# Summing the weighted experts of the last three groups on VectorE in one operation each, instead of on GpSimd in three additions

## The chip, the cores and the metric

The kernel runs on one core of a Trainium2 chip. The metric is the device time of one execution in microseconds (us), the median of several runs. The core's engines work side by side, each through its own list of instructions in order, and they wait for one another on semaphores: TensorE (PE in the profile) for matrix products, VectorE (DVE), ScalarE (ACT), GpSimd (POOL), and SyncE (SP), which here only issues DMAs.

## What is computed

An image of 160 x 160 tokens with 64 channels goes through one block: attention along each row, then a mixture of experts for each token. Cut to what matters:

```python
x = x + attention(layernorm(x))            # 4 heads of 32, a bias from the tokens, gates
t = to_tokens(x)                           # 25600 tokens of 64 channels
h = layernorm(t)
router_probs = softmax(h @ router_w + router_b)            # 8 experts
top_p, top_i = top_k(router_probs, 2)
top_p = top_p / sum(top_p)
expert_out = einsum("bnd,edc->bnec", h, expert_w) + expert_b
out = t + einsum("bnk,bnkc->bnc", top_p, gather(expert_out, top_i))
```

The kernel computes all 8 experts of every token and weights them with a table of coefficients that holds zero for the six that were not chosen. Summing the 8 weighted experts of a token is the part that the change touches.

## The kernel before

The 160 rows of the image are cut into 40 groups (GROUPS) of 4 rows, that is 640 tokens: 5 slabs (T, numbered t) of 128 tokens, one token to a partition. A first phase of about 80 us normalizes all tokens. After it every engine runs the same written list of steps, n = -2 to 43. In step n an engine works on up to six groups at different stages: the scores of group n and n+1, the attention output of group n-1, router, coefficients and the first experts of group n-2, the other experts of group n-3, and the result of group n-4. The list in each engine's own `step(n, a)` is the order; nothing reorders it. From step 37 on the steps are written out (they are not in the loop), and from step 40 on no new group comes in, so a step holds less and less: group 37 ends in step 41, group 38 in step 42, group 39, the last, in step 43. These last steps are called the drain here.

The way of one group g through its last stages:

- `attention_out` (VectorE, L864) adds the projected attention to the input: x1. `total2` (L870) and `mean2` (L875) follow, GpSimd's `center` (L395) subtracts the mean, ScalarE squares, `sumsq2` (VectorE, L882) sums, GpSimd's `norm2` takes the power (L376) and multiplies (L379), ScalarE and `low2` (GpSimd, L406) make the halves, and TensorE turns them over (`turn2`, L1004). ScalarE copies them out, and TensorE computes the router and the experts of the slabs.
- `logits` (VectorE, L889), twelve small operations `route` (L898 to L910), an exponential on ScalarE, and `share` 1 to 5 (L921 to L928) give the coefficients. All are chained: each waits for the one ahead.
- `weigh` (VectorE, L944) multiplies the 8 x 64 experts' values of a slab, read from PSUM, by the coefficients, into a buffer `prod` in SBUF. Slab 2 takes another way: ScalarE copies it to `kept`, and GpSimd weighs it (`weigh_kept`, L423).
- GpSimd sums the 8 experts of a slab in three additions, 8 to 4 (`mix_halves`, L429), 4 to 2 (L434) and 2 to 1 (L436), both in `mix_rest`; the sum goes to `ymix`.
- `residual` (GpSimd, L443) adds x1 and the five slabs of ymix to `base`. `finish` (VectorE, L953) adds the experts' bias, and SyncE stores the result.

Two more things on GpSimd's list matter below: `og_low` (L417) makes the low halves of the gated attention output, without which TensorE cannot project it (`project_out`, L1236 to L1238), and `residual`. In the list of a step both stand behind the additions of the step before. VectorE's gated outputs come from `gated` (L849) and `normed` (L857), and TensorE's spreading of the inverse sums stands between these two.

Of the kernel before, what the change touches and what calls it, by code (L numbers as in the profile page):

```python
# [5 lines left out]
ALU = mybir.AluOpType  # L6
ACT = mybir.ActivationFunctionType
AX = mybir.AxisListType
# [37 lines left out]
def build(nc, x, Wq, Wk, Wv, Wg, Wo, Wb, router_w, router_b, expert_w, expert_b, mask, out):  # L46
    with ExitStack() as ctx:
# [145 lines left out]
        def pairs_loop(eng, body, first, end):  # L193

            with eng.Fori(0, (end - first) // 2) as i:
                body(i * 2 + first, first % 2)
                body(i * 2 + (first + 1), 1 - first % 2)
# [23 lines left out]
        def on(g):  # L221

            return not isinstance(g, int) or 0 <= g < GROUPS

        def later(g):

            return on(g) and not (isinstance(g, int) and g == 0)

        N_WLOAD = 2 * 6 + 1 + T + 3 * T


        @KE.sync
        def _(sp):
            def at(g, size):

                return g * size if isinstance(g, int) else sp.snap(g * size)

            def load_x(m, a):
                start = at(m, 2 * TG * D)
                need(sp, lnA, 3 * m - 3)  # L240
                sp.dma_start(xin[a][:], x_flat[bass.ds(start, 2 * TG * D)].rearrange("(p t d) -> p t d", p=P, t=T2)
                             ).then_inc(x_loaded[a], 16)

            def keep_xs(m, a):
                start = at(m, 2 * TG)
                sp.wait_ge(xs_made, m + 1)
                sp.dma_start(xs_all[:, bass.ds(start, 2 * TG)], xs_pair[a][:]).then_inc(xs_kept[a], 16)

            for m in range(2):
                load_x(m, m)  # L250
            for half_ in range(2):
                sp.dma_start(w_raw[64 * half_:64 * half_ + 64, B0:B0 + 4], Wb).then_inc(wb_loaded, 16)
            ld = lambda dst, src: sp.dma_start(dst, src).then_inc(w_loaded, 16)

            for half_ in range(2):
                rows = slice(64 * half_, 64 * half_ + 64)
                ld(w_raw[rows, V0:V0 + 128], Wv)
                ld(w_raw[rows, G0:G0 + 128], Wg)
                ld(w_raw[rows, X0:X0 + 512].rearrange("p (e c) -> p e c", e=E), expert_w.rearrange("e d c -> d e c"))
                ld(w_raw[rows, R0:R0 + 8], router_w)  # L260
                ld(w_raw[rows, Q0:Q0 + 128], Wq)
                ld(w_raw[rows, K0:K0 + 128], Wk)
                load_x(2 + half_, half_)
            ld(w_raw[:, O0:O0 + 64], Wo)
            load_x(4, 0)
            for t in range(T):
                ld(rb[:, t, :], router_b.rearrange("(a e) -> a e", a=1).broadcast_to([P, E]))
            load_x(5, 1)
            keep_xs(0, 0)
            load_x(6, 0)  # L270
            keep_xs(1, 1)
            sp.wait_ge(const_ready, 1)

            def load_eb(part):
                for t in range(T):
                    ld(eb_raw[40 * part + 8 * t:40 * part + 8 * t + 8, t, :], expert_b)

            load_eb(0)
            load_x(7, 1)
            keep_xs(2, 0)  # L280
            load_eb(1)
            load_x(8, 0)
            keep_xs(3, 1)
            load_eb(2)

            def load_xq(g, a):
                start = at(g, TG)
                for k in range(2):
                    for c in range(2):
                        need(sp, qk_done[k][c], g - 1)  # L290
                sp.dma_start(xs_q[a][:], xs_all[:, bass.ds(start, TG)]).then_inc(xq_loaded[a], 16)

            def load_xv(g, a):
                start = at(g, TG)
                need(sp, v_done, g - 1)
                need(sp, vr_done, g - 1)
                for c in range(2):
                    need(sp, g_done[c], g - 1)
                sp.dma_start(xs_v[a][:], xs_all[:, bass.ds(start, TG)]).then_inc(xv_loaded[a], 16)

            def phase1(n, a):
                load_x(n + 2, a)
                keep_xs(n - 3, 1 - a)

            pairs_loop(sp, phase1, 7, PAIRS - 3)
            for n in range(PAIRS - 3, PAIRS + 4):
                if n + 2 < PAIRS: load_x(n + 2, n % 2)
                if n - 3 < PAIRS: keep_xs(n - 3, 1 - n % 2)
                if n == PAIRS:
                    sp.wait_ge(xs_kept[0], 16)  # L310
                    for g in range(2):
                        load_xq(g, g)
            def load_res(g, a):
                start = at(g, TG * D)
                need(sp, x1_done, g - 1)
                sp.dma_start(xin[a][:, 0:T], tokens(x_flat, start)).then_inc(x_loaded[a], 16)

            def store(g, a):
                start = at(g, TG * D)
                sp.wait_ge(res_done, g + 1)  # L320
                sp.dma_start(tokens(out_flat, start), res[a][:]).then_inc(res_stored[a], 16)

            for a in range(2):
                sp.wait_ge(xs_kept[a], 16 * (PAIRS // 2))
            load_xv(0, 0)
            load_res(0, 0)
            load_xv(1, 1)
            load_res(1, 1)

            def step(n, a):  # L330
                b = 1 - a
                if on(n + 3): load_xq(n + 3, b)
                if isinstance(n, int) and n < 1: return
                if on(n + 1): load_xv(n + 1, b)
                if on(n - 4): store(n - 4, a)
                if on(n + 1): load_res(n + 1, b)

            for n in range(-1, LOOP):
                step(n, n % 2)
            pairs_loop(sp, step, LOOP, LOOP_END)  # L340
            for n in range(LOOP_END, LAST):
                step(n, n % 2)
            for a in range(2):
                sp.wait_ge(res_stored[a], 16 * (GROUPS // 2))

# [2 lines left out]
        def _(pool):  # L348
# [95 lines left out]

            def step(n, a):
                b = 1 - a
                if on(n - 4): mix_rest(n - 4, 3)
                if on(n - 4): mix_rest(n - 4, 4)
                if on(n - 2): og_low(n - 2, 1)
                if on(n - 2): og_low(n - 2, 0)  # L450
                if on(n - 4): residual(n - 4, a)
                if on(n - 1): rinv_low(n - 1)
                if on(n - 3): mix_halves(n - 3, 0)
                if on(n - 2): center(n - 2, a)
                if on(n - 3): weigh_kept(n - 3, 2)
                if on(n - 2): norm2(n - 2, a)
                if on(n - 3): mix_halves(n - 3, 1)
                if on(n - 2): low2(n - 2, a)
                if on(n - 3): mix_rest(n - 3, 1)
                if on(n - 3): mix_rest(n - 3, 0)  # L460
                if on(n - 3): mix_halves(n - 3, 2)
                if on(n - 3): mix_halves(n - 3, 3)
                if on(n - 3): mix_rest(n - 3, 2)
                if on(n - 3): mix_halves(n - 3, 4)

            run_steps(pool, step)

# [191 lines left out]
        def _(dve):  # L659
# [276 lines left out]
            def weigh(g, t, bank):  # L936
# [6 lines left out]
                else: need(dve, mix_step[WEIGHED[i::2][-1]], 3 * (g - 1) + 1)  # L943
                dve.scalar_tensor_tensor(out=prod_of(t)[:], in0=bank[:].rearrange("p (e c) -> p e c", e=E), scalar=1.0 / UP,  # L944
                                         in1=coef[:, t, :].unsqueeze(2).broadcast_to([P, E, D]),
                                         op0=ALU.mult, op1=ALU.mult).then_inc(prod_done[t], 1)

            def finish(g, a, bank):

                dve.wait_ge(cb_done, g + 1)  # L950
                dve.wait_ge(base_done, g + 1)
                need(dve, res_stored[a], 8 * g - 8 * a)
                dve.scalar_tensor_tensor(out=res[a][:], in0=bank[:, 0:T * D].rearrange("p (t d) -> p t d", t=T), scalar=1.0 / UP,  # L953
                                         in1=base[:], op0=ALU.mult, op1=ALU.add).then_inc(res_done, 1)

            def step(n, a):
# [5 lines left out]
                if on(n - 1): normed(n - 1, 0, ps_x)  # L962
                if on(n - 1): normed(n - 1, 1, ps_o)
                if on(n - 3): weigh(n - 3, 3, ps_m)
                for k in range(6, 8):
                    if on(n - 3): share(n - 3, k)
                if on(n - 3): weigh(n - 3, 4, ps_o)
                if later(n + 2): qk_low(n + 2, a, 1, 0, ps_m)
                if later(n + 2): qk_low(n + 2, a, 0, 0, ps_x)
                if on(n + 1): row_max(n + 1, 1)  # L970
# [15 lines left out]
                    if on(n - 2): share(n - 2, k)  # L986
                if on(n - 1): total2(n - 1, b)
                if on(n - 2): weigh(n - 2, 0, ps_m)
                if on(n - 1): mean2(n - 1, b)
                if later(n + 2): qk_low(n + 2, a, 0, 1, ps_x)  # L990
                if on(n + 2): row_max(n + 2, 0)
                if on(n - 1): sumsq2(n - 1, b)
                if on(n - 2): weigh(n - 2, 1, ps_r)

            run_steps(dve, step)


# [340 lines left out]
```

## Time and profile before

| what | value |
|---|---|
| median of three runs | 909.1 us (908.54 to 911.25) |
| the profiled execution | 911.06 us, its span 909.2 us |
| mean granted TensorE clock | 0.974 of full speed |
| VectorE busy | 760.7 us, 84% of the span |
| GpSimd busy | 641.0 us, 71% of the span |
| TensorE busy | 812.7 us, 89% of the span |

The span reaches from the first to the last instruction of the trace; all times of instructions below are counted from its start. In the steps of the middle a step takes about 19 us. The drain takes up the last 45 us.

### The profile page before, as it was taken

The page shows a single profiled execution, that of the slowest core. Times are in us where ns is not written, and L with a number is a line of the kernel's source. Part 1 is how long each engine was busy: PE and PEld are TensorE (multiplying, and loading weights), DVE is VectorE, ACT ScalarE, POOL GpSimd, SP SyncE. Part 2 cuts the span into 40 slices and gives each one's busy share as a digit, 9 for nine tenths or more (in the row PEclk, how much of TensorE's full clock was granted, in tenths as well). Part 3 has the DMA queues.
Part 4 walks back from the last instruction along what each step waited for, and adds up shares of the span by engine and source line. Part 5 has one row for each costly group of instructions (what it writes and reads, how often), then busy time and mean ns, then how long its engine had stood idle before and what let it go on. Part 6 is the DMA issues. An engine that isn't in the chain of part 4 may idle for free.

```text
span 909.2 us, 40901 instructions
## 1 busy us (share of the span) xinstructions
PE 812.7 (89%) x15532; PEld 536.6 (59%) x15532; DVE 760.7 (84%) x1818; ACT 485.4 (53%) x1049; POOL 641.0 (71%) x1029
## 2 busy tenths in 40 slices
PE   1999678999999999999999999999999999999743
PEld 1898345656656566665666656666666666656421
DVE  8998445898898898988989989899888998898764
ACT  3886235555565555655456554555546555565410
POOL 6994002677777677776777767777677777777786
PEclk9999989999999999999999999999999999999975
DMA  4563000011110011001110011100101001100000
GB/s 126 192 197 134 19 18 25 25 31 54 39 32 30 29 50 36 29 29 34 45 36 29 29 39 40 36 29 29 45 34 36 29 29 50 36 23 25 17 14 16
DMA packets 32461, 40.82 MB, mean 45 GB/s; under 512 B 6288, under 2 KB 27280, under 8 KB 32400
## 3 DMA queue, kind: packets, MB, share of 16 engines
q1 hardware_dynamic: 31920, 39.95, 13.3%
q8 instruction: 43, 0.70, 0.3%
q14 instruction: 18, 0.15, 0.1%
q10 hardware_dynamic: 480, 0.02, 0.0%
HBM read 13.74 MB, written 6.55 MB: 22 GB/s over the span
## 4 chain that ended last, share of the span: by engine, by line
PE 36%; DVE 35%; issue 19%; POOL 7%; ACT 1%; DVEq 1%; DMA 0%; POOLq 0%; ACTq 0%
DVE negm L826 6%; PE psS L1113 6%; DVE rinv L842 5%; PE psS L1088 5%; DVE prod L944 3%; POOL ln_s L376 3%; PE ps_o L1170 3%; PE ps_x L1173 2%; PE ps_x L1170 2%; PE ps_o L1173 2%; DVE og L857 2%; DVE rt L906 2%; DVE q_lo L778 2%; POOL xn L379 2%; DVE ogu L849 2%
## 5 line engine op out<-in xcount | busy, mean ns | idle before, releaser
L429 POOL TENSOR_TENSOR add<-prod 128x256 f32<-128x256 f32 x160 | 116.5, 728 | 100.4 <-DVE prod L944 100.4
L826 DVE TENSOR_REDUCE negm<-psS 128x12 f16<-128x1920 f32 x80 | 146.0, 1825 | 12.8 <-PE psS L1098 7.9
L376 POOL TENSOR_TENSOR ln_s<-ln_s,half 128x5 f32<-128x5 f32 (+1 forms) x60 | 86.2, 1436 | 38.6 <-DVE ln_s L882 30.8
L434 POOL TENSOR_TENSOR add<-add 128x128 f32<-128x128 f32 x200 | 91.4, 457 | 0.1
L602 ACT ACTIVATE hl<-xn 128x320 f16<-128x320 f32 x40 | 18.8, 470 | 129.4 <-POOL xn L379 129.4
L546 ACT ACTIVATE pt_b<-psS 128x1920 f32<-128x1920 f32 x40 | 70.9, 1771 | 18.9 <-PE psS L1132 15.1
L411 POOL TENSOR_TENSOR rinv_lo<-rinv,rinv_hi 128x160 f16<-128x160 f32 x40 | 19.8, 496 | 83.8 <-ACT rinv_hi L577 83.8
L436 POOL TENSOR_TENSOR ymix<-add 128x64 f32<-128x64 f32 x200 | 64.4, 322 | 15.7
L1088 PE MATMUL psS<-bm,ident 128*128 128x480 f16 (+1 forms) x320 | 68.4, 336 | 7.0 <-ACT pt_a L546 3.1
L417 POOL TENSOR_TENSOR og_lo<-og,og_hi 128x320 f16<-128x320 f32 x80 | 61.8, 794 | 17.0 <-ACT og_hi L583 17.0
L1113 PE MATMUL psS<-bt_hi,ident 128*128 128x320 f16 (+1 forms) x320 | 68.5, 337 | 2.3 <-DVE negm L826 2.3
L857 DVE TENSOR_TENSOR og<-ogu,ps_x 128x320 f32<-128x320 f32 x40 | 19.5, 487 | 51.5 <-issue 48.9
L553 ACT ACTIVATE v_main<-ps_x 128x512 f32<-128x512 f32 x40 | 23.9, 598 | 65.9 <-PE ps_x L1184 65.9
L379 POOL TENSOR_TENSOR xn<-xc,ln_s 128x320 f32<-128x320 f32 (+1 forms) x60 | 54.2, 904 | 5.3 <-POOL ln_s L376 1.1
L1113 PE MATMUL psS<-bt_lo,ident 128*128 128x320 f16 x320 | 57.7, 303 | 0.0
L596 ACT ACTIVATE sq<-xc 128x320 f32<-128x320 f32 x40 | 18.9, 471 | 72.0 <-POOL xc L395 72.0
L944 DVE SCALAR_TENSOR_TENSOR prod<-ps_m,coef 128x512 f32<-128x512 f32 x80 | 54.7, 684 | 2.8 <-PE ps_m L1246 2.7
L1236 PE MATMUL ps_m<-w_hi,og_hi 128*128 128x64 f16 x200 | 28.1, 208 | 30.1 <-DVE rinv L842 22.4
L546 ACT ACTIVATE pt_a<-psS 128x1280 f32<-128x1280 f32 x40 | 49.5, 1237 | 3.8 <-PE psS L1122 3.8
L1088 PEld LDWEIGHTS psS<-bm,ident 128*128 128x128 f16 x320 | 27.2, 98 | 36.6 <-ACT pt_a L546 22.1
L842 DVE RECIPROCAL rinv<-ps_m 128x160 f32<-128x160 f32 x40 | 45.8, 1145 | 1.7 <-PE ps_m L1146 1.7
L1236 PEld LDWEIGHTS ps_m<-w_hi,og_hi 128*128 128x128 f16 x200 | 24.0, 128 | 37.4 <-DVE rinv L842 18.7
(279 smaller groups left out, 2979.5 us busy)
## 6 DMA issues: line engine op xcount, KB each, us to landing
xin<-in_x SPq DMA_DIRECT2D x20, 320.0 KB, 3.0
xs_all<-xs_pair SPq DMA_DIRECT2D x20, 320.0 KB, 2.5
xs_q<-xs_all SPq DMA_DIRECT2D x40, 160.0 KB, 2.1
xs_v<-xs_all SPq DMA_DIRECT2D x40, 160.0 KB, 2.1
xin<-in_x SPq DMA_DIRECT2D x40, 160.0 KB, 2.2
out<-res SPq DMA_DIRECT2D x40, 160.0 KB, 1.8
w_raw<-in_expert_w SPq DMA_DIRECT2D x2, 128.0 KB
eb_raw<-in_expert_b SPq DMA_DIRECT2D x15, 2.0 KB
```

Source lines behind the costliest of these rows:

```text
L376: pool.tensor_tensor(ln_s[a][:, 3, 0:w], ln_s[a][:, 2, 0:w], half[:, 0:w], ALU.pow).then_inc(own, 1)
L379: pool.tensor_tensor(xn[a][:, 0:w], xc[a][:, 0:w], ln_s[a][:, 3, 0:w].unsqueeze(2).broadcast_to([P, w, D]), ALU.mult).then_inc(own, 1)
L417: pool.tensor_tensor(og_lo[:, cols], og[:, cols], og_hi[:, cols], ALU.subtract).then_inc(ogl_done[c], 1)
L429: pool.tensor_tensor(add1[t % 2][:], prod_of(t)[:, 0:4, :], prod_of(t)[:, 4:8, :], ALU.add).then_inc(mix_step[t], 1)
L434: pool.tensor_tensor(add2[t % 2][:], add1[t % 2][:, 0:2, :], add1[t % 2][:, 2:4, :], ALU.add).then_inc(mix_step[t], 1)
L436: pool.tensor_tensor(ymix[:, t, :], add2[t % 2][:, 0, :], add2[t % 2][:, 1, :], ALU.add).then_inc(mix_step[t], 1)
L546: act.activation(pt[:].rearrange("p h s i -> p h (s i)"), psS[:, :, 0:slots * N], ACT.Exp).then_inc(exp_done[c], 1)
L826: dve.tensor_reduce(negm[c][:, :, 0:slots], psS[:, :, 0:slots * N].rearrange("i h (s j) -> i h s j", s=slots), AX.X, ALU.max, negate=True) ...
L842: dve.reciprocal(rinv[:], bank[:, 0:N]).then_inc(rinv_done, 1)
L944: dve.scalar_tensor_tensor(out=prod_of(t)[:], in0=bank[:].rearrange("p (e c) -> p e c", e=E), scalar=1.0 / UP, in1=coef[:, t, :].unsqueeze ...
L1088: mm(psS[:, h, 0:(3 - c) * N], lhsT=ident16[:], rhs=bm3[:, h].rearrange("i s j -> i (s j)")[:, 0:(3 - c) * N], start=True, stop=False)
L1113: mm(psS[:, h, 0:wide], lhsT=ident16[:], rhs=part[:, h].rearrange("j s i -> j (s i)")[:, 0:wide], start=part is bt3_hi, stop=False)
```

## The change

For groups 37, 38 and 39 (`late(g)`), GpSimd's `mix_halves` and `mix_rest` are left out. In their place VectorE sums a slab by one `tensor_reduce` over the experts (`mix_late`), which reads the buffer through a rearranged view, with the expert innermost. The weighted values of one token lie in SBUF as 8 rows of 64 floats, so neighbouring reads of this view are 64 floats (256 bytes) apart. `mix_late` counts the slab's semaphore up by 3, as the three additions did. `weigh_kept` of slab 2 stays on GpSimd. The edits to SyncE's part only write the same list in another way.

```diff
+        LATE = GROUPS - 3
+        def late(g):
+            return isinstance(g, int) and LATE <= g < GROUPS
+        def early(g):
+            return on(g) and not late(g)
...
 # GpSimd's step
-                if on(n - 4): mix_rest(n - 4, 3)
-                if on(n - 4): mix_rest(n - 4, 4)
+                if early(n - 4): mix_rest(n - 4, 3)
+                if early(n - 4): mix_rest(n - 4, 4)
...
-                if on(n - 3): mix_halves(n - 3, 0)
+                if early(n - 3): mix_halves(n - 3, 0)
...
 # VectorE
+            def mix_late(g, t):
+                dve.wait_ge(prod_done[t], g + 1)
+                need(dve, base_done, g)
+                dve.tensor_reduce(ymix[:, t, :], prod_of(t)[:].rearrange("p e c -> p c e"), AX.X, ALU.add).then_inc(mix_step[t], 3)
...
                 if on(n - 3): weigh(n - 3, 3, ps_m)
+                if late(n - 3): mix_late(n - 3, 3)
                 for k in range(6, 8):
                     if on(n - 3): share(n - 3, k)
                 if on(n - 3): weigh(n - 3, 4, ps_o)
+                if late(n - 3): mix_late(n - 3, 4)
+                if late(n - 3): mix_late(n - 3, 2)
...
                 if on(n - 2): weigh(n - 2, 0, ps_m)
+                if late(n - 2): mix_late(n - 2, 0)
...
                 if on(n - 2): weigh(n - 2, 1, ps_r)
+                if late(n - 2): mix_late(n - 2, 1)
```

What this does to the lists of instructions is shown at two places. First GpSimd, from the `low2` of group 39 in step 41 to the end of its list. Before:

```order
L406 TENSOR_TENSOR hl<-xn,hl 128x5x64
L434 TENSOR_TENSOR add<-add 128x128
L436 TENSOR_TENSOR ymix<-add 128x64
...
L443 TENSOR_TENSOR base<-ymix,x_0 128x320
L429 TENSOR_TENSOR add<-prod 128x256
L423 TENSOR_TENSOR kept<-kept,coef 128x512
L429 TENSOR_TENSOR add<-prod 128x256
L434 TENSOR_TENSOR add<-add 128x128
...
L443 TENSOR_TENSOR base<-ymix,x_1 128x320
```

In the changed kernel (line numbers are 8 higher there):

```order
L414 TENSOR_TENSOR hl<-xn,hl 128x5x64
L451 TENSOR_TENSOR base<-ymix,x_0 128x320
L431 TENSOR_TENSOR kept<-kept,coef 128x512
L451 TENSOR_TENSOR base<-ymix,x_1 128x320
```

All additions L429, L434 and L436 of these groups are gone, 15 to a group; both `residual` (base) have nothing ahead of them any more but what VectorE delivers.

Second VectorE, from the last coefficients of group 39 in step 41 to the end of its list. In the changed kernel, where L952 is `weigh`, L960 the new sum, L967 `finish`, L939 and L941 are `share` 6 and 7:

```order
L936 TENSOR_TENSOR coef<-rt,rs 128x40
L952 SCALAR_TENSOR_TENSOR prod<-ps_m,coef 128x512
L960 TENSOR_REDUCE ymix<-prod 128x64
L952 SCALAR_TENSOR_TENSOR prod<-ps_r,coef 128x512
L960 TENSOR_REDUCE ymix<-prod 128x64
L967 SCALAR_TENSOR_TENSOR res<-ps_m,base 128x320
L952 SCALAR_TENSOR_TENSOR prod<-ps_m,coef 128x512
L960 TENSOR_REDUCE ymix<-prod 128x64
L939 CAST c_stack<-coef 128x2x40
L941 TENSOR_TENSOR c_stack<-coef,c_stack 128x40
L952 SCALAR_TENSOR_TENSOR prod<-ps_o,coef 128x512
L960 TENSOR_REDUCE ymix<-prod 128x64
```

One more L960 (of `kept`) and the last `finish` follow. Before, the same list stands there without the five sums. In steps 39 and 40 the sums stand in the same places behind their `weigh`, so that what follows in the list, `mean2`, `gated`, `share` and `logits` among it, comes behind them.

## Rows read from the trace of the kernel before

**Rows 1.** The page's first part: busy us, share of the span, instructions.

```profile
PE 812.7 (89%) x15532; PEld 536.6 (59%) x15532; DVE 760.7 (84%) x1818; ACT 485.4 (53%) x1049; POOL 641.0 (71%) x1029
```

**Rows 2.** The chain of work that ended last: start us, us, what.

```profile
900.22 0.44 PE ps_m L1259 x5
900.66 5.76 issue
906.42 0.49 DVE res L953
```

**Rows 3.** Timeline of GpSimd in the drain: start, us, line, out<-in, idle before.

```profile
863.84 0.72 POOL L395 TENSOR_TENSOR xc<-x,ln_s 128x320 f32<-128x320 f32 x1
...
875.16 1.56 POOL L417 TENSOR_TENSOR og_lo<-og,og_hi 128x320 f16<-128x320 f32 x2
...
880.30 0.72 POOL L429 TENSOR_TENSOR add<-prod 128x256 f32<-128x256 f32 x1 [2.76 <-DVE prod L944]
880.99 0.72 POOL L395 TENSOR_TENSOR xc<-x,ln_s 128x320 f32<-128x320 f32 x1
...
892.57 0.86 POOL L443 TENSOR_TENSOR base<-ymix,x 128x320 f32<-128x320 f32 x1 [0.26 <-POOL ymix L436]
...
904.25 0.32 POOL L436 TENSOR_TENSOR ymix<-add 128x64 f32<-128x64 f32 x1
905.12 0.86 POOL L443 TENSOR_TENSOR base<-ymix,x 128x320 f32<-128x320 f32 x1 [0.55 <-POOL ymix L436]
```

**Rows 4.** Timeline of VectorE in the drain, with the same columns.

```profile
862.98 0.16 DVE L875 TENSOR_SCALAR ln_s<-ln_s 128x5 f32<-128x5 f32 x1
...
869.87 0.68 DVE L944 SCALAR_TENSOR_TENSOR prod<-ps_o,coef 128x512 f32<-128x512 f32 x1
871.55 0.20 DVE L889 TENSOR_TENSOR lg<-ps_x,rb 128x40 f32<-128x40 f32 x1 [1.01 <-PE ps_x L1226]
...
876.27 0.48 DVE L921 TENSOR_SCALAR rs<-rs 128x5 f32<-128x5 f32 x1 [0.28 <-ACT rs L615]
876.78 0.19 DVE L922 RECIPROCAL rs<-rs 128x5 f32<-128x5 f32 x1
877.83 0.49 DVE L864 SCALAR_TENSOR_TENSOR x<-ps_m,xin 128x320 f32<-128x320 f32 x1 [0.86 <-PE ps_m L1238]
...
879.53 0.69 DVE L944 SCALAR_TENSOR_TENSOR prod<-ps_m,coef 128x512 f32<-128x512 f32 x1 [0.20 <-PE ps_m L1246]
880.14 0.16 DVE L875 TENSOR_SCALAR ln_s<-ln_s 128x5 f32<-128x5 f32 x1
...
885.47 0.82 DVE L931 CAST c_stack<-coef 128x80 f16<-128x80 f32 x1
...
889.28 0.20 DVE L889 TENSOR_TENSOR lg<-ps_x,rb 128x40 f32<-128x40 f32 x1 [1.99 <-PE ps_x L1226]
...
892.63 0.85 DVE L909 TENSOR_TENSOR rt<-rt,rs 128x40 f32<-128x40 f32 x1
...
893.96 0.17 DVE L921 TENSOR_SCALAR rs<-rs 128x5 f32<-128x5 f32 x1 [0.27 <-ACT rs L615]
...
899.27 0.68 DVE L944 SCALAR_TENSOR_TENSOR prod<-ps_o,coef 128x512 f32<-128x512 f32 x1
```

**Rows 5.** Stretches of VectorE from `logits` to `share` 1 (steps 40, 41): us, busy (instructions), clock.

```profile
871.55:876.27 4.72, 4.03 (x14) 0.65 0.00 0
889.28:893.96 4.68, 4.00 (x14) 0.50 0.01 4
```

**Rows 6.** All 40 instructions of one line of `route`: ns min/median/max, first and last start.

```profile
L909 DVE TENSOR_TENSOR rt<-rt,rs x40: 199/200/850, 165.1 to 892.6; 128x40 f32<-128x40 f32 x40
```

**Rows 7.** VectorE's reductions by shape: count, busy us, mean ns, idle before.

```profile
L870 DVE TENSOR_REDUCE ln_s<-x 128x5 f32<-128x320 f32 x40 | 19.2, 480 | 0.0
...
L734 DVE TENSOR_REDUCE ln_s<-xin 128x10 f32<-128x640 f32 x20 | 16.3, 814 | 1.7 <-DMA xin<-in_x 1.5
...
L685 DVE TENSOR_REDUCE fold<-ident 128x32 f32<-128x128 f32 x1 | 0.4, 356 | 0.0
```

More of the change, by code:

```diff
@@ L227, in later, with third_on @@
             return on(g) and not (isinstance(g, int) and g == 0)
+        LATE = GROUPS - 3
[3 more added lines that the diff above has]
+            return on(g) and not late(g)
+        def third_on(g):
+            return on(g) and not (isinstance(g, int) and g < 2)
         N_WLOAD = 2 * 6 + 1 + T + 3 * T
@@ L331, in step @@
                 b = 1 - a
-                if on(n + 3): load_xq(n + 3, b)
-                if isinstance(n, int) and n < 1: return
-                if on(n + 1): load_xv(n + 1, b)
+                if third_on(n + 3): load_xq(n + 3, b)
+                if third_on(n + 1): load_xv(n + 1, b)
                 if on(n - 4): store(n - 4, a)
[L336 to L342, printed above, removed]
+                if third_on(n + 1): load_res(n + 1, b)
+            run_steps(sp, step)
             for a in range(2):
@@ L456, in step @@
                 if on(n - 2): norm2(n - 2, a)
-                if on(n - 3): mix_halves(n - 3, 1)
+                if early(n - 3): mix_halves(n - 3, 1)
                 if on(n - 2): low2(n - 2, a)
[L459 to L464, printed above, removed]
+                if early(n - 3): mix_rest(n - 3, 1)
+                if early(n - 3): mix_rest(n - 3, 0)
+                if early(n - 3): mix_halves(n - 3, 2)
+                if early(n - 3): mix_halves(n - 3, 3)
+                if early(n - 3): mix_rest(n - 3, 2)
+                if early(n - 3): mix_halves(n - 3, 4)
             run_steps(pool, step)
```

## The prediction

> **What bounds the kernel now.** I read four views, from the whole to the end of the program. The page's first part shows TensorE, VectorE and GpSimd busy for 89%, 84% and 71% of the span [rows 1]; these are averages over all steps, and the change touches only the last three groups. Nothing ahead of 863 us moves: the first new sum stands in step 39, behind the `weigh` that `mean2` at 862.98 follows. So the question is what sets the time of the last 45 us.
>
> The chain of work that ended last closes with TensorE's bias product at 900.22, a piece called "issue" of 5.76 us, and the last `finish` at 906.42 [rows 2]. The piece is not idle in truth. GpSimd's timeline shows what runs beside it: the last of the additions of group 39 starts at 904.25 and `residual` at 905.12, for 0.86 us [rows 3]. VectorE's last `weigh` began at 899.27 [rows 4], so 7.15 us pass from there to `finish`, and GpSimd fills them.
>
> GpSimd's queue shows a second wait. The additions of group 37 stand ahead of `og_low`, which starts at 875.16 [rows 3]. TensorE's projection waits for it, and VectorE's `attention_out` sits idle for 0.86 us before 877.83 [rows 4]. Elsewhere in the drain the path runs through VectorE: a round goes from `logits` over `route` and `share`, `attention_out`, `weigh`, `mean2`, then GpSimd's `center` and norm, TensorE's turn and router, to the next `logits` at 889.28 [rows 4]. The last group is VectorE alone from 889.28 to 899.27.
>
> The third thing to see is the small operations of `route`. One has a median of 200 ns over 40 executions, but a maximum of 850 ns, at 892.6 [rows 6]. That one starts at 892.63 and ends at 893.48, while GpSimd's `residual` runs from 892.57 to 893.43 [rows 3, 4]: it ends right behind it. So an operation on two SBUF operands is held up by GpSimd's work, and a GpSimd with nothing to do will make this chain shorter.
>
> **The cost of one sum.** No row shows it. VectorE's reductions over contiguous floats take 480 ns for 320 elements and 814 ns for 640 [rows 7]: 1.044 ns an element and 0.147 us fixed. For 512 elements that is 0.68 us, the lower bound. The only reduction that reads across rows is `fold`, 32 outputs of 4 elements that lie 128 bytes apart: 356 ns for 128 elements [rows 7], where the line gives 281. The excess of 75 ns can be fixed (then the sum takes 0.76), by output (64 in place of 32, 0.83) or by element (512 in place of 128, 0.98). Which one, a single row doesn't tell. I take the middle, 0.83 us, and keep 0.68 and 0.98 for the range. Below is left open: a gain under 0.68 would need a reduction faster than the contiguous one.
>
> The Trainium skill speaks against the change here: Advanced Engine Details and Errata, section Memory Cachelines, says that SBUF has lines of 16 bytes, and that reads which change the line each time pay a penalty. It gives no size for VectorE. By GPSIMD Engine Reference, section Performance pitfalls for Q7 kernels, a wide step costs GpSimd half as much again per element; put on VectorE, which the page does not claim, an estimate of 0.95 us and an end about 1.8 us later than by my value.
>
> In the queue a sum costs a little more than its duration. Behind a `weigh` the next operation starts 0.61 us after its start (879.53 to 880.14 [rows 4]), before its end. The sum must wait for the end (0.69), starts 0.03 later, and lets the next one in 0.08 before its own end: 0.83 + 0.03 = 0.86 us more. The sum of slab 2 follows another sum and depends on older work: 0.75 us. There are fifteen, five a group.
>
> **The sum, along the path.** Shifts are against the trace of before.
> - Step 39. `mean2` comes 0.86 later, at 863.84. Before, `center` waited behind an addition of GpSimd and started at 863.84 [rows 3]. Now nothing is ahead, and it starts 0.16 + 0.08 behind `mean2`: 864.08, +0.24. The norm follows at +0.24. The sum of slab 1 stands ahead of `gated`, so `gated`, TensorE's spreading and `normed` go to +1.10.
> - Step 40. Slab 3's sum makes that +1.96, so the `weigh` of 869.87 starts at 871.83. Then 0.61 + 0.86 + 0.75 until VectorE is free: `logits` at 874.05 where it was 871.55. Of 3.57 us of extra work since the norm 1.01 us fell into idle time [rows 4]; +2.50.
> - From `logits` to `share` 1 VectorE took 4.72 us [rows 5]. Undisturbed it is 12 x 0.235 (200 ns and the step to the next [rows 6]) + 0.17 + 0.27 = 3.26. With `share` 1, 0.48 in place of 0.17 [rows 4], 1.76 us were lost to GpSimd. One collision stays: `residual` now starts when slab 2's sum is done, and so meets `route`'s second operation; I put it at 0.65, as in the 850 ns row. Relief 1.11, shift +1.39 at `share` 2.
> - `og_low` of group 39 now runs behind ScalarE's high half at about 872 instead of 875.16, and TensorE's projection is done before VectorE asks. `attention_out`'s idle time goes: 876.78 + 1.39 + 0.11 = 878.28, +0.45 instead of +1.39. `weigh` has +0.45, `mean2` +1.31 (881.45), and `center`, which had waited for the addition at 880.30 and started at 880.99 [rows 3], goes to 881.69, +0.70.
> - Step 41. Slab 1's sum: `finish` of group 37, the experts behind it on TensorE, and `weigh` of slab 3 at +1.56. Slab 3's sum +2.42. `share` 6, 0.82 us in the trace [rows 4], takes 0.20 undisturbed, and `share` 7 gives 0.10: +1.70. Slabs 4 and 2 end 1.61 later, but 1.99 us of idle time stand before `logits` [rows 4]; it starts at 890.54, +1.26. TensorE's router, which waits for the bank that slab 4's `weigh` frees, would be ready at 890.5 as well.
> - `route` of group 39: 4.68 [rows 5] against 3.26, less the collision: relief 0.77, shift +0.49. Sums of slabs 0 and 1: +2.21 at `finish` of group 38, TensorE's experts and `weigh` of slab 3. Slab 3's sum and `share`: +2.97. The `weigh` of 899.27 is at 902.24.
> - The end. Slab 4's sum ends at 902.24 + 0.69 + 0.03 + 0.83 = 903.79, slab 2's at 904.54. `residual` starts 0.26 later (as behind the additions before 892.57), takes 0.86, and `finish` starts 0.44 behind it (905.98 to 906.42 [rows 3, 4]): 906.10 against 906.42.
>
> So 7.15 us at the end become 3.86, a gain of 3.29 us, and 2.97 us are paid ahead of it: **0.3 us faster**. The profiled execution had a span of 909.2 and 911.06 us in all, 1.9 us more; what lies around the span isn't touched, so I take the difference off the median of 909.1: **908.8 us**. Each sum lies on the path once VectorE's idle times are used up, so the end moves by 15 times what the sum differs from 0.83: 0.15 us for each 10 ns.
>
> Semaphores: the new wait on `base_done` asks for the `residual` one group back. For group 37 this is done at about 860, for 38 at about 875 and for 39 at about 892; the sums of slab 0 come at 863, 880 and 896, so it is never late. If it were, `mean2` and everything behind it would wait.
>
> **The rivals.**
> - Stride free: the sum takes 0.68 us, as a contiguous one. For it: `fold` ran in the first 5 us, once, and its excess may be fixed. 15 x 0.15 = 2.25 more: 906.5 us. Chance 0.27, with a fixed excess (0.76, 907.7) in it.
> - By element: 0.98 us, 15 x 0.15 = 2.25 more than forecast: 911.1 us. Chance 0.22.
> - Half rate, the case that ends slower: each read of another row costs two reads, 0.147 + 512 x 2.088 ns = 1.22 us. 15 x 0.39 = 5.8 later: 914.6 us. `fold` speaks against it, since by the same rule it should take 414 ns and took 356. From 1.03 us on the end is over 0.3% later. Chance 0.10.
> - No relief: the small operations stay slow although GpSimd stands still. Then 1.11 + 0.77 + 0.72 + 0.10 = 2.7 us are not returned: 911.5 us. The row at 892.63 speaks against it. Chance 0.06.
> - The forecast, with a sum of 0.80 to 0.90 us: 908.3 to 909.9. Chance 0.35.
>
> The rule of cache lines is the ground of the second and third case; taken as full line changes at each read it would be the third, 914.6 us.
>
> **How the numbers follow.** A change under 0.3%, 2.7 us, can't be told from none here. Faster than that needs a sum of at most 0.67 us, or that `residual` meets no operation of `route` (another 1.3 us): 0.20, mostly from the first rival. Slower needs 1.03 us, or the by-element case together with lost relief: 0.16. The same: 0.64. The range takes in both bounds of the sum and about 0.7 us beyond them for the medians' own spread: 905.8 to 911.8.
>
> **What would show it.** A row L960 with the duration, 0.83 us; fifteen of them. `center` at 864.1 and 881.7, `logits` at 874.1 and 890.5, the stretches to `share` 1 near 3.9 us in place of 4.7, `og_low` at about 872, no idle time before `attention_out`, last `weigh` at 902.2, last `finish` at 906.1. I am wrong if the sum takes under 0.7 or over 1 us, if `route` doesn't get shorter, or if TensorE or ScalarE is late behind the moved `weigh`.

## The result and the profile after

The changed kernel takes 912.02 us (median of 20 runs, 910.29 to 915.29) against 909.65 us for the kernel before (20 runs): ratio 1.003, 95% interval 1.0019 to 1.004. It is 2.4 us slower. The forecast was 908.8 us and a range of 905.8 to 911.8, so the time lies just outside the range, and it moved the other way.

The profiled execution took 913.7 us with a span of 911.8 us. It reached the first `weigh` of group 37 at 862.63, 0.26 us later than before, which is ahead of the first instruction that the change adds. To compare the drains I count from the start of that `weigh` to the start of the last `finish`. Before it is 862.37 (0.61 us ahead of `mean2` at 862.98) to 906.42 [rows 4]: 44.05 us. After it is 862.63 to 909.08: 46.45 us. The difference, 2.40 us, is the whole difference of the medians.

VectorE's groups of the drain after the change, by line and shape: count, busy us and mean ns, idle before.

```profile
L960 DVE TENSOR_REDUCE ymix<-prod 128x64 f32<-128x512 f32 x12 | 12.3, 1025 | 1.1
L952 DVE SCALAR_TENSOR_TENSOR prod<-ps_m,coef 128x512 f32<-128x512 f32 x6 | 4.2, 692 | 3.0 <-PE ps_m L1265 2.8
L960 DVE TENSOR_REDUCE ymix<-kept 128x64 f32<-128x512 f32 x3 | 3.0, 1013 | 0.0
```

The new sum takes 1.02 us, not 0.83. Against 44.05 us that difference is small, but it comes fifteen times: 15 x 0.19 = 2.9 us. The forecast gain of 0.3 us and the loss of 2.4 us lie 2.7 us apart.

The timeline of VectorE after the change, the rows that answer to [rows 4]: start, us, line, out<-in, idle before.

```profile
862.63 0.69 DVE L952 SCALAR_TENSOR_TENSOR prod<-ps_m,coef 128x512 f32<-128x512 f32 x1 [0.28 <-PE ps_m L1265]
863.41 1.10 DVE L960 TENSOR_REDUCE ymix<-prod 128x64 f32<-128x512 f32 x1
864.43 0.16 DVE L883 TENSOR_SCALAR ln_s<-ln_s 128x5 f32<-128x5 f32 x1
...
871.07 0.69 DVE L952 SCALAR_TENSOR_TENSOR prod<-ps_m,coef 128x512 f32<-128x512 f32 x1 [0.27 <-PE ps_m L1265]
...
875.79 0.19 DVE L897 TENSOR_TENSOR lg<-ps_x,rb 128x40 f32<-128x40 f32 x1
...
879.88 0.49 DVE L872 SCALAR_TENSOR_TENSOR x<-ps_m,xin 128x320 f32<-128x320 f32 x1
...
890.14 0.19 DVE L939 CAST c_stack<-coef 128x80 f16<-128x80 f32 x1
...
893.13 0.19 DVE L897 TENSOR_TENSOR lg<-ps_x,rb 128x40 f32<-128x40 f32 x1
...
905.21 0.68 DVE L952 SCALAR_TENSOR_TENSOR prod<-ps_o,coef 128x512 f32<-128x512 f32 x1
905.98 1.02 DVE L960 TENSOR_REDUCE ymix<-prod 128x64 f32<-128x512 f32 x1
906.91 1.00 DVE L960 TENSOR_REDUCE ymix<-kept 128x64 f32<-128x512 f32 x1
909.08 0.49 DVE L967 SCALAR_TENSOR_TENSOR res<-ps_m,base 128x320 f32<-128x320 f32 x1 [1.17 <-issue]
```

Three things are to be seen. From the last `weigh` to `finish` there are now 3.87 us instead of 7.15: 3.28 us gained where they were looked for. The idle time ahead of both `logits` and of `attention_out` is gone. And the last `weigh` comes at 905.21 instead of 899.27, 5.7 us later after the offset of 0.26: 5.7 - 3.3 = 2.4 us.

The two stretches from `logits` to `share` 1, which answer to [rows 5]: us, VectorE's busy time (instructions), granted clock, DMA share, GB/s.

```profile
875.79:879.57 3.78, 3.10 (x14) 0.50 0.00 0
893.13:896.90 3.77, 3.09 (x14) 0.50 0.02 7
```

They are 0.9 us shorter than before (4.72 and 4.68), with the same instructions. One collision stayed in each, in `route`'s second operation, as GpSimd's timeline shows beside VectorE's. VectorE first:

```profile
893.58 0.76 DVE L907 TENSOR_TENSOR rt<-lg,rs 128x40 f32<-128x40 f32 x1
```

GpSimd, same columns:

```profile
864.66 0.72 POOL L403 TENSOR_TENSOR xc<-x,ln_s 128x320 f32<-128x320 f32 x1 [3.99 <-DVE ln_s L883]
...
873.95 1.55 POOL L425 TENSOR_TENSOR og_lo<-og,og_hi 128x320 f16<-128x320 f32 x2 [4.11 <-ACT og_hi L591]
...
893.43 0.86 POOL L451 TENSOR_TENSOR base<-ymix,x 128x320 f32<-128x320 f32 x1 [4.80 <-DVE ymix L960]
```

`residual` ends at 894.29, the operation on VectorE at 894.34, and it took 0.76 us in place of 0.20.

One wait is new: the `weigh` of slab 3 at 871.07 waited 0.27 us for TensorE, and its counterpart before, at 868.77, did not wait. TensorE's timeline shows the experts' product that it waits for, in parts of 512 columns. Before:

```profile
867.99 0.38 PE L1245 MATMUL ps_m<-w_hi,xs 128*128 128x512 f16 x1
```

After, with the idle time of TensorE that stands ahead of it:

```profile
869.36 0.24 PE L1174 MATMUL ps_x<-rinv_hi,row_to_all 128*128 128x160 f16 x1 [3.98 <-DVE ogu L857]
...
869.97 0.63 PE L1264 MATMUL ps_m<-w_hi,xs 128*128 128x512 f16 x1
```

The granted clock from 870 to 872 us was 1.00 before (the level of 2.4 GHz) and 0.50 after (1.2 GHz); before, it fell only between 872 and 874 us (0.75 there, 0.50 from 874 on). TensorE had waited 3.98 us for VectorE's gated outputs, which now come behind the sum of slab 1; before it had waited 2.31 us at this place.

### The profile page after: what moved, and what is told of

It is laid out like the page before. It is cut to its first block and busy times, and to the rows that moved or that the text cites. A ratio compares the mean times of both kernels' runs of the same rounds, so it can differ in the third digit from the quotient of the medians.

```text
span 911.8 us, 40886 instructions
## 1 busy us (share of the span) xinstructions
PE 814.7 (89%) x15532; PEld 537.1 (59%) x15532; DVE 772.1 (85%) x1833; ACT 485.4 (53%) x1049; POOL 619.6 (68%) x984
## 5 line engine op out<-in xcount | busy, mean ns | idle before, releaser
L437 POOL TENSOR_TENSOR add<-prod 128x256 f32<-128x256 f32 x148 | 107.9, 729 | 92.6 <-DVE prod L952 92.6
L442 POOL TENSOR_TENSOR add<-add 128x128 f32<-128x128 f32 x185 | 84.7, 458 | 0.0
L444 POOL TENSOR_TENSOR ymix<-add 128x64 f32<-128x64 f32 x185 | 59.6, 322 | 14.5
L952 DVE SCALAR_TENSOR_TENSOR prod<-ps_m,coef 128x512 f32<-128x512 f32 x80 | 54.7, 684 | 3.0 <-PE ps_m L1265 2.8
L431 POOL TENSOR_TENSOR kept<-kept,coef 128x512 f32<-128x512 f32 x40 | 41.9, 1046 | 3.9 <-DVE coef L936 3.9
```

Source lines behind the costliest of these rows:

```text
L437: pool.tensor_tensor(add1[t % 2][:], prod_of(t)[:, 0:4, :], prod_of(t)[:, 4:8, :], ALU.add).then_inc(mix_step[t], 1)
L442: pool.tensor_tensor(add2[t % 2][:], add1[t % 2][:, 0:2, :], add1[t % 2][:, 2:4, :], ALU.add).then_inc(mix_step[t], 1)
L444: pool.tensor_tensor(ymix[:, t, :], add2[t % 2][:, 0, :], add2[t % 2][:, 1, :], ALU.add).then_inc(mix_step[t], 1)
```

## The experiments

All ratios are to the kernel before, run beside it on the same chip.

**1. The disputed cost by itself.** Behind the last `finish` of the changed kernel a row of single operations is appended, each waiting for the one ahead. Its core:

```diff
+            by = lambda v, a, s: v.rearrange("p (a e s) -> p a s e", a=a, s=s)
+            dst = lambda a, s: bench_out[:, 0:a * s].rearrange("p (a s) -> p a s", a=a)
+            for _ in range(2):
+                for s_ in (1, 2, 4, 16, 64):
+                    alone(dve.tensor_reduce(dst(64 // s_, s_), by(w_raw[:, 0:512], 64 // s_, s_), AX.X, ALU.add))
+                for s_ in (32, 128):
+                    alone(dve.tensor_reduce(bench_out[:, 0:s_], w_raw[:, 0:4 * s_].rearrange("p (r c) -> p c r", r=4), AX.X, ALU.add))
+                alone(dve.tensor_reduce(bench_out[:, 0:64], ps_x[:].rearrange("p (c e) -> p c e", e=8), AX.X, ALU.add))
+                alone(dve.tensor_reduce(bench_out[:, 0:64], ps_x[:].rearrange("p (e c) -> p c e", e=8), AX.X, ALU.add))
...
+                alone(dve.scalar_tensor_tensor(out=bench_out[:].rearrange("p (c e) -> p c e", e=E), in0=ps_x[:].rearrange("p (e c) -> p c e", e=E),
+                                               scalar=1.0 / UP, in1=across, op0=ALU.mult, op1=ALU.mult))
+                alone(dve.scalar_tensor_tensor(out=bench_out[:].rearrange("p (c e) -> p e c", e=E), in0=ps_x[:].rearrange("p (e c) -> p e c", e=E),
+                                               scalar=1.0 / UP, in1=along, op0=ALU.mult, op1=ALU.mult))
```

The last two are the weighing, first with PSUM read 64 floats apart and SBUF written in a row, then with PSUM read in a row and SBUF written 8 floats apart.

> The changed kernel with a row of single operations appended on VectorE after the last result, each waiting for the one ahead: sums of 512 elements whose neighbouring reads lie 1, 2, 4, 16 and 64 floats apart, two of 4 deep (128 and 512 elements, 32 and 128 floats apart), the same from PSUM, the three additions, and the weighing written with the expert innermost. Theory (a price for each element whose read lies far from the one before): 0.68 us at a distance of 1 float, about 1.0 us at 64, and 4 deep the same price by element: 0.36 us for 128 and about 1.0 us for 512. Rival (a price by output): 512 elements 4 deep have 128 outputs and take more than 1.1 us, and the price grows with the number of outputs at one distance. Rival (a fixed price or one of waiting): the contiguous sum takes about 0.9 us here too. Where the price sets in with the distance is open; if lines of 16 bytes make it, 1 and 2 floats are free or nearly, and 4, 16 and 64 cost the same. Its time as a whole means nothing.

Measured, first the sums from SBUF. The line with all ten sums of 512 elements, ns min/median/max; the shortest is a contiguous one:

```profile
L1028 DVE TENSOR_REDUCE bench_out<-w_raw x10: 675/1008/1057, 907.0 to 921.0; 128x64 f32<-128x512 f32 x10
```

Then what the chain of waits gives for each: start, us. The rows are, in order, reads 2, 4, 16 and 64 floats apart (512 elements), and 4 deep with 128 and with 512 elements. These pieces are up to 0.02 us longer than the operations themselves: in the second round of the same row the contiguous sum and the one at 2 floats took 686 ns each.

```profile
907.70 0.70 DVE bench_out L1028
...
908.42 1.06 DVE bench_out L1028
...
909.51 1.02 DVE bench_out L1028
...
910.55 1.02 DVE bench_out L1028
...
911.59 0.38 DVE bench_out L1030
...
912.00 1.03 DVE bench_out L1030
```

And the timeline for PSUM (contiguous, then 64 floats apart) and for the weighing (PSUM read apart; then SBUF written apart):

```profile
913.05 0.69 DVE L1031 TENSOR_REDUCE bench_out<-ps_x 128x64 f32<-128x512 f32 x1
913.78 0.69 DVE L1032 TENSOR_REDUCE bench_out<-ps_x 128x64 f32<-128x512 f32 x1
...
915.55 0.69 DVE L1038 SCALAR_TENSOR_TENSOR bench_out<-ps_x,coef 128x512 f32<-128x512 f32 x1
916.27 1.07 DVE L1040 SCALAR_TENSOR_TENSOR bench_out<-ps_x,coef 128x512 f32<-128x512 f32 x1
```

The price is one by element. The 4-deep sums have 32 and 128 outputs, and the second takes the same time as the sum with 64 outputs of 8: the number of outputs plays no part. (1.02 - 0.147) / 512 = 1.71 ns an element against 1.04 for contiguous ones. It sets in between a distance of 2 floats (0.69 us) and 4 floats (1.06), and does not grow to 64. From PSUM nothing is paid for the distance; writes to SBUF 8 floats apart cost as much as reads do (1.07 us against 0.69). The Trainium skill, Advanced Engine Details and Errata, section Memory Cachelines, says that SBUF has lines of 16 bytes and that a line needs at least two hits to absorb the access latency. A step of 8 bytes gives a line two hits and one of 16 bytes gives it one; the trace agrees, with 0.69 against 1.06 us.

**2. Contiguous reads.** Since PSUM may be read apart for nothing, `weigh` can turn the order over while it reads PSUM, and the sum finds each token's experts side by side. Slabs 0, 1, 3 and 4 of the last three groups:

```diff
+                if late(g):
+                    dve.scalar_tensor_tensor(out=turned(prod_of(t)), in0=bank[:].rearrange("p (e c) -> p c e", e=E), scalar=1.0 / UP,
+                                             in1=coef[:, t, :].unsqueeze(1).broadcast_to([P, D, E]), ...)
...
-                dve.tensor_reduce(ymix[:, t, :], prod_of(t)[:].rearrange("p e c -> p c e"), AX.X, ALU.add).then_inc(mix_step[t], 3)
+                dve.tensor_reduce(ymix[:, t, :], turned(prod_of(t)) if t not in KEPT else prod_of(t)[:].rearrange("p e c -> p c e"), AX.X, ALU.add).then_inc(mix_step[t], 3)
```

> For slabs 0, 1, 3 and 4 of the last three groups the weighing writes prod with the expert innermost (reading PSUM 64 floats apart), and the sum reads it contiguously. Slab 2 as in the change. Theory (the distance of the reads in SBUF is what made the sum 1.02 us): L960 on prod falls to 0.68 us, and if the weighing still takes 0.68 us, twelve sums save 12 x 0.34 = 4.1 us: about 908 us, 0.2% under the kernel before. Rival (the price moves to the weighing, since its reads or writes now lie apart): weigh goes to 1.0 us and the time stays at 912. Rival (the sum costs 1.02 us however it reads): 912 as well, weigh unchanged.

Measured: 907.74 us against 909.92, ratio 0.9974 (0.9964 to 0.9984). The groups of the drain:

```profile
L966 DVE TENSOR_REDUCE ymix<-prod 128x64 f32<-128x512 f32 x12 | 8.2, 686 | 1.1
L954 DVE SCALAR_TENSOR_TENSOR prod<-ps_m,coef 128x512 f32<-128x512 f32 x6 | 4.1, 691 | 2.6 <-PE ps_m L1271 2.4
```

The sum takes 0.69 us and `weigh` what it took. Twelve sums, each 0.34 us cheaper, are 4.1 us; the drain is 42.05 us (861.96 to 904.01) against 46.45, 4.4 us less. With this one cost taken away the change is 2.2 us faster than the kernel before instead of 2.4 slower. The first rival is out, and so is the second.

**3. No sums at all.** The sum is replaced by a no-operation that counts the semaphore; ymix of the last three groups is not computed.

```diff
-                dve.tensor_reduce(...).then_inc(mix_step[t], 3)
+                dve.nop().then_inc(mix_step[t], 3)
```

> The changed kernel without its fifteen sums (a no-operation counts the semaphores instead; ymix of the last three groups is not computed). Neither engine sums these groups. Theory (the sums are all on the path once VectorE's idle times are used up, and GpSimd's absence itself makes the drain shorter): the logits come about 3 us earlier than before at group 39, route takes 0.8 to 1.4 us less per group, the last finish stands 2 us behind the last weigh; in all 8 to 9 us under the kernel before, 900 to 902 us. Rival (GpSimd's additions cost the rest of the drain nothing, only the last 7 us are theirs): 904 us or more, with route as long as before.

Measured: 902.39 us against 909.92, ratio 0.9918 (0.9902 to 0.9934), 7.5 us less, a little short of the 8 to 9 that were expected. The rival, 904 us or more with `route` as long as before, is out. The drain is 36.76 us (861.35 to 898.11), 9.7 us under that of the changed kernel, though the fifteen sums take 15.3 us. So a part of them costs nothing on the path: the idle time ahead of both `logits` is back, 0.93 and 2.02 us, and the next instruction starts 0.09 us before a sum ends. The no-operations are not free either, since they still wait for the end of each `weigh`. The first of the two stretches to `share` 1 took 4.41 us, since `og_low` ran at 870.33, inside it; the second took 3.22 us, the 3.26 of an undisturbed one.

**4. GpSimd kept busy.** The sums stay on VectorE, and GpSimd makes the same fifteen additions a group at their old places, on data that nobody reads.

```diff
                 if early(n - 3): mix_halves(n - 3, 0)
+                if late(n - 3): idle_adds(n - 3, 0, 0)
...
+            def idle_adds(g, t, part):
+                pool.wait_ge(prod_done[t], g + 1)
+                ... # part 0: one addition of 256 columns; part 1: one of 128, one of 64
```

> The changed kernel with its sums on VectorE, and GpSimd doing the same fifteen additions a group again at their old places, on data of their own that nobody reads. Theory (relief is real): route, share 6 and the idle time before attention_out come back, 2.5 to 3 us, and GpSimd's additions behind the last weigh set the end again (7.15 us from weigh to finish in place of 3.9), 3.3 us: 917 to 918.5 us. Rival (VectorE's small operations do not depend on GpSimd): only the 3.3 us of the end, 915.3 us, and route at 4.0 us.

Measured: 914.37 us against 909.92 in four runs, ratio 1.0045 (1.0028 to 1.0062), where the changed kernel had 1.003. The drain of the profiled execution is 48.74 us against 46.45, 2.3 us longer. The relief is real, but this run gives only a part of it back: no wait ahead of `attention_out` returned, and not all of `route`. The number that I gave was 917 to 918.5, mostly because I expected 3.3 us more at the end, and they did not come: from the last `weigh` (909.00) to `finish` (912.90) it took 3.90 us, as in the changed kernel. VectorE's sums hold its `weigh`s so far apart that GpSimd's additions keep up with them: `residual` starts at 911.95, as VectorE's last sum ends. Windows of VectorE for the same two stretches as above:

```profile
877.84:882.29 4.45, 3.77 (x15) 0.50 0.00 0
896.78:900.56 3.78, 3.10 (x14) 0.50 0.01 4
```

Only the first got longer again (0.67 us); in the second GpSimd had finished its additions. `share` 6 and 7 of group 38 took 0.65 us each instead of 0.19 and 0.20, which is 0.9 us more. The rest of the 2.3 us, 0.5 us, lies ahead of the first `logits`, and 0.2 us behind the second. The rival, that these operations do not depend on GpSimd, is out by these rows; its time, 915.3 us, lies inside the interval of the four runs.

**5. Slab 2 contiguous too.** ScalarE copies it out of PSUM turned over, GpSimd weighs it so.

```diff
+                if late(g):
+                    act.activation(turned(kept), bank[:].rearrange("p (e c) -> p c e", e=E), ACT.Copy, scale=1.0 / UP)
```

> As the run with contiguous reads, and slab 2 as well: ScalarE copies it out of PSUM with the expert innermost, GpSimd weighs it there, and VectorE's sum of it reads contiguously. Theory (each sum is worth its whole duration on the path): L969's three rows fall from 1.01 to 0.69 us, 3 x 0.33 = 1.0 us less than with slab 2 left as it was: ratio 0.9963 to the kernel before. Rival (the sum of slab 2 is partly hidden, since TensorE's router is ready no earlier than VectorE): 0 to 0.4 us, ratio 0.9974.

Measured: 906.87 us against 909.42, ratio 0.9975 (0.9966 to 0.9984): no different from experiment 2. The three sums fell from 1.01 to 0.68 us, and the drain from 42.05 to 41.56 us (862.51 to 904.07). VectorE now waits again ahead of `logits` of group 38:

```profile
873.78 0.20 DVE L905 TENSOR_TENSOR lg<-ps_x,rb 128x40 f32<-128x40 f32 x1 [0.16 <-PE ps_x L1258]
```

This is the rival's case, in a small part: TensorE's router sets that point once VectorE is fast enough. More was lost in `route` of this group, where GpSimd held up two operations (0.44 and 0.79 us) and the stretch to `share` 1 took 4.06 us (873.78 to 877.84) in place of 3.78 in experiment 2. So 0.5 of the 1.0 us shows in the drain, and none in the medians. GpSimd's weighing of the turned slab took 1.26 us in place of 1.04, which nobody waited for.

**6. and 7. Two slabs only, behind the last `weigh`.** From the kernel before: VectorE sums slabs 3 and 4, both behind `weigh` of slab 4, read contiguously; GpSimd keeps 0, 1 and 2. For the last group alone, and for the last three.

```diff
+        ON_V = (3, 4)
+        def early(g, t):
+            return on(g) and not (late(g) and t in ON_V)
...
                 if on(n - 3): weigh(n - 3, 4, ps_o)
+                if late(n - 3): mix_late(n - 3, 4)
+                if late(n - 3): mix_late(n - 3, 3)
```

> The kernel before, with only the last group's slabs 3 and 4 summed on VectorE, both behind the last weigh, read contiguously; slabs 0, 1 and 2 and all other groups on GpSimd. Theory (sums ahead of the last weigh are all cost, sums behind it share the 7.15 us with GpSimd): nothing moves ahead of the last weigh, VectorE sums until 1.9 to 2.1 us behind its start and GpSimd until 2.3 to 2.5, finish 3.7 to 3.9 us behind it: 3.3 us faster than before, ratio 0.9964. Rival (GpSimd's path sets the end through slab 2 and not through slabs 3 and 4): under 2 us.

> The same split for groups 37, 38 and 39. For 37 and 38 the two sums fall into VectorE's idle time ahead of logits (1.01 and 1.99 us in the kernel before), and GpSimd has 3 us less to do in each, so that route is disturbed for a shorter time and the low halves of group 39 come before attention_out asks. Theory (idle time takes the sums, relief is paid in full): 3.3 us of the end, 0.9 us of attention_out's wait, 0.5 to 1 us a group of route: 5 to 6 us faster than before, ratio 0.9935 to 0.9945. Rival (relief comes only when GpSimd is quite idle): as with the last group alone, ratio 0.9964.

Measured: for the last group 906.33 us against 909.42, ratio 0.9969 (0.9956 to 0.9981). The last `weigh` starts at 898.60 and `finish` at 902.26, 3.66 us behind it: the whole gain is at the end, 7.15 - 3.66 = 3.5 us. The rival, a gain under 2 us, is out. For three groups 904.26 us, ratio 0.9944 (0.993 to 0.9958), within what was expected. In its timeline the two sums (1.28 us together) stand where VectorE had waited:

```profile
885.35 1.28 DVE L968 TENSOR_REDUCE ymix<-prod 128x64 f32<-128x512 f32 x2
887.25 0.20 DVE L900 TENSOR_TENSOR lg<-ps_x,rb 128x40 f32<-128x40 f32 x1 [0.62 <-PE ps_x L1250]
```

Of the 1.99 us of idle time ahead of that `logits` 0.62 are left. The idle time of `attention_out` (0.86 us before) is gone. The relief in `route` came for group 39 alone: its stretch to `share` 1 took 3.87 us in place of 4.68, that of group 38 4.73 us, as long as before (4.72). The rival, 0.9964, lies outside the interval.

**8. The change for the last group alone.** Five slabs, reads 64 floats apart.

```diff
-        LATE = GROUPS - 3
+        LATE = GROUPS - 1
```

> The change as made, but for group 39 alone (all five slabs, strided reads). Theory (three sums of 1.09 us ahead of the last weigh, against 3.3 us at the end, and the relief in share): the last weigh comes 3.1 us later, finish 3.9 us behind it, within 0.3 us of the kernel before: ratio 0.9998. The change's loss then comes from groups 37 and 38, 2.4 to 2.8 us together. Rival (each group pays alike): a third of the change's loss, ratio 1.001.

Measured: 910.63 us against 909.42, ratio 1.0008 (0.9999 to 1.0018). The interval holds the rival's 1.001 and just misses the 0.9998 of the theory. The profiled execution speaks the other way: its drain took 43.75 us (861.00 to 904.75), 0.3 us less than before, as the theory has it. But it is one of five runs at 908.5 to 909.4 us, while the other six took 910.6 to 911.7, and no trace shows one of these. So it stays open how the loss divides among the groups.

**9. The mean ahead of the first addition.** Experiment 7, and in steps 40 and 41 GpSimd runs `center` ahead of its first addition of slab 0.

```diff
+                if late(n - 3) and on(n - 2): center(n - 2, a)
                 if early(n - 3, 0): mix_halves(n - 3, 0)
-                if on(n - 2): center(n - 2, a)
+                if on(n - 2) and not late(n - 3): center(n - 2, a)
```

> As the split over three groups, and in steps 40 and 41 GpSimd subtracts the mean (center) ahead of its first addition of slab 0 and not behind it. Theory (center waited 0.6 us for that addition in each round, which is why mean2 coming 0.86 us later cost the change only 0.24 there): center starts 0.08 us behind mean2, and each of the two rounds is 0.6 us shorter: 1.2 us less than the split, ratio 0.9931 to the kernel before. Rival (the weighing of slab 2, which follows center and takes 1.04 us, or ScalarE's square sets the norm's start): no gain, ratio 0.9944.

Measured: 903.15 us against 909.7, ratio 0.9926 (0.9909 to 0.9942), the lowest of the kernels that compute everything. The interval overlaps that of experiment 7 (0.993 to 0.9958), so what this step adds is read from the traces. `mean2` and the sum of squares of group 39 on VectorE, then the weighing of slab 2 and the norm (`norm2`) on GpSimd:

```profile
876.76 0.16 DVE L887 TENSOR_SCALAR ln_s<-ln_s 128x5 f32<-128x5 f32 x1
878.26 0.49 DVE L894 TENSOR_REDUCE ln_s<-sq 128x5 f32<-128x325 f32 x1 [1.33 <-ACT sq L608]
878.36 1.04 POOL L434 TENSOR_TENSOR kept<-kept,coef 128x512 f32<-128x512 f32 x1
879.36 1.17 POOL L387 TENSOR_TENSOR ln_s<-ln_s,half 128x5 f32<-128x5 f32 x1
```

The same in experiment 7:

```profile
878.11 0.16 DVE L886 TENSOR_SCALAR ln_s<-ln_s 128x5 f32<-128x5 f32 x1
880.21 0.49 DVE L893 TENSOR_REDUCE ln_s<-sq 128x5 f32<-128x325 f32 x1 [1.94 <-ACT sq L607]
879.64 1.04 POOL L434 TENSOR_TENSOR kept<-kept,coef 128x512 f32<-128x512 f32 x1
880.79 1.18 POOL L387 TENSOR_TENSOR ln_s<-ln_s,half 128x5 f32<-128x5 f32 x1
```

The sum of squares comes 1.50 us behind `mean2` in place of 2.10. The norm hardly gains by it: it starts 2.60 us behind `mean2` in place of 2.68. The addition of slab 0 still stands ahead of it in GpSimd's list, and so does the weighing of slab 2, which now ends 0.65 us behind the sum of squares. About the norm the rival was right; in the changed kernel, where the addition is gone, the norm starts 2.06 us behind `mean2` (864.43 to 866.49). The drain is 37.80 us (860.82 to 898.62) against 38.65 in experiment 7 (861.39 to 900.04), 0.85 us of the 1.2 that were expected, and it comes from elsewhere. From `mean2` to the next `logits` the first round is 0.47 us shorter (8.37 against 8.84), since no wait stands ahead of these `logits` and VectorE's own list, which the sum of squares heads, sets them; the second is 0.08 us shorter. Other operations of `route` were held up in group 38, which makes its stretch 4.42 us in place of 4.73.

## Why the prediction was wrong

- **The term that was mis-sized is the cost of one sum.** I took the middle of three readings of one row, `fold`: 0.83 us. The sum took 1.02 us. The reading by element gave 0.98, and experiment 1 shows that it is the right one: 0.38 us for 128 elements and 1.03 for 512, both 4 deep. By my own slope, 15 x 0.19 = 2.85 us turn 0.3 us of gain into 2.5 us of loss, and the measured loss is 2.4. Experiment 2 makes twelve of the fifteen reads contiguous and shortens the drain by 4.4 us.
- **Smaller terms nearly cancel, and that is luck.** The hand-over from `weigh` to the sum was 0.78 us from start to start and not 0.72 (0.69 + 0.03): 12 x 0.06 = 0.7 us more. The wait for TensorE at 871.07, for which the sum had no term, is 0.3 us more; the prediction had named it only among the signs of being wrong. Against this the end was cheaper by 0.4 us: from the end of the last sum (907.91) to `finish` 1.17 us and not 1.56. And the relief was larger by 0.7 us. With the sum that makes -0.3 + 2.85 + 0.7 + 0.3 - 0.4 - 0.7 = 2.5 us of loss, for 2.4 measured.
- **The relief was real and undersized.** The prediction had 1.11 + 0.77 + 0.72 + 0.10 = 2.7 us. Read from the two traces: `logits` to `share` 2 took 3.98 us in both groups, in place of 5.23 (871.55 to 876.78) and 4.88 (889.28 to 894.16); from the start of `share` 6 to the `weigh` behind it 0.80, 0.27 and 0.15 us less went by for groups 38, 39 and 37. That is 3.4 us. Experiment 4, where GpSimd's additions meet fewer of these operations, gives 2.3 us of it back. The rival without relief is out.
- **The path was right.** With the sum at 1.02 and the hand-over as measured, `center` of group 39 comes at 881.69 + 6 x 0.19 + 5 x 0.06 = 883.1 and its `logits` at 890.54 + 10 x 0.19 + 8 x 0.06 = 892.9. The trace has, less the offset of 0.26, 883.2 (883.45) and 892.9; up to there the wait for TensorE and the larger relief offset each other. `center` of group 38, forecast 0.24 late with a sum of 0.83, came 0.56 late (864.66 less 0.26, against 863.84) with one of 1.10. One sentence of the prediction was too strong: the last group is not VectorE alone, since the `weigh` of slab 3 waits 1.13 us for TensorE in both kernels; the sum of terms carried that stretch unchanged, so it made no difference. `og_low` was forecast at about 872 and came at 873.95. ScalarE makes the high half first, and in its list the copy of the turned slabs stands ahead of that: it started at 872.45 and not at 869.84 as before, behind TensorE's turn (`turn2`) at the low clock. Nobody waited for `og_low`.
- **The rivals.** What happened is the one by element, 911.1 us, to which I gave 0.22. Stride free and half rate are out by the row of 1.02 us. The upper end of the range took that rival's 911.1 and 0.7 us on top. The 0.2 us beyond it say little by themselves: I had counted from 909.1 us, the median of three runs, and the kernel before had 909.65 over twenty. Against that base the loss is 2.4 us where the rival had 2.0. I had placed the limit for a slowdown that shows at a sum of 1.03 us, close to what came.
- Not foreseen: that the sum's order could be turned over for nothing on the way out of PSUM. I took the price of the far reads as given with the change.

## What to carry to other kernels

Count how often a new operation comes in a row on one engine before choosing a value for it: here 0.2 us on each of fifteen decided the sign. Where a single row is the only witness, each reading of it is to be carried to the end as a case of its own. Moving work from the engine that ends last to another pays most where the other has nothing to do, behind its last own operation and in its waits: with contiguous reads, five slabs a group on VectorE gained 2.2 and 2.6 us (experiments 2 and 5), and the two slabs that fall into such places 5.2 us (experiment 7). A reduction over a middle axis from SBUF can be prepared by whoever writes the tile from PSUM: here reads of PSUM 64 floats apart took VectorE no longer than contiguous ones. And a wait that gets shorter is worth only what the next instruction in the list behind it gains, as experiment 9 shows.

## What the hardware did that was not expected

VectorE reads of float32 from SBUF cost 1.04 ns an element at distances of 4 and 8 bytes and 1.7 ns at 16, 64 and 256 bytes (0.68, 0.69, 1.06, 1.02 and 1.02 us for 512 elements). Writes to SBUF 32 bytes apart cost the same (1.07 us), PSUM reads 256 bytes apart nothing (0.69 us). VectorE's sum was not held up by GpSimd: with GpSimd's additions beside it (experiment 4) it took a mean of 1.03 us, while `share` 7, 40 columns with both operands in SBUF, went from 0.20 to 0.65 us, and `share` 6, a cast of 80 columns, from 0.19 to 0.65. TensorE's granted clock fell to the lower level about 3 us earlier in the changed kernel, after a wait of 3.98 us, and the experts' products of 512 columns behind it took 0.63 us in place of 0.38.
